# Perceiver layer on one core: turned probabilities spread by sixteen SBUF-to-SBUF transfers instead of through a DRAM buffer

## The reference, cut to what matters

```
x = x + cross_attention(layernorm(x), ctx)     # 256 queries, 25088 context rows, width 512
x = x + attention(layernorm(x))                # 16 heads
x = x + ffn(layernorm(x))                      # shared expert + 1 of 32 routed experts per token

scores   = einsum('bqh,bkh->bqk', Q_char, K_sub) * scale      # 256 x 25088
char2sub = einsum('bqk,bkh->bqh', softmax(scores), V_sub)
```

## Time and profile before

| | |
|---|---|
| time, median of 3 executions | 1302.32 us (1300.58 to 1302.76) |
| the profiled execution | 1300.58 us, its span 1298.8 us |
| mean granted TensorE clock | 0.957 |
| PE busy / DVE / ACT | 85% / 45% / 30% of the span |
| the loop over pairs, first `spread` to last | 74.89 to 660.92 us of the span |

### The profile page before, as it was taken

How to read it: one execution, slowest core, us unless ns; L and a number is a source line. 1 busy time by engine, 2 the same in 40 slices (tenths; PEclk the granted TensorE clock), 3 DMA queues, 4 the chain that set the end, 5 groups by cost and what they waited for, 6 DMA issues and landing times.

```text
span 1298.8 us, 16532 instructions
## 1 busy us (share of the span) xinstructions
PE 1105.0 (85%) x6586; PEld 750.9 (58%) x6586; DVE 582.5 (45%) x859; ACT 392.5 (30%) x621; POOL 3.5 (0%) x20
## 2 busy tenths in 40 slices
PE   8999888998999899999889989999886675665666
PEld 8777666776777777777666945766332222222223
DVE  2466666776776777677664245421110010010101
ACT  1245434554553554455441225211110000000000
POOL 1000000000000000000000000000000000000000
PEclk9999999999999999999989989999998989889998
DMA  9168887787777877878762811897899999999996
GB/s 357 59 227 291 278 276 278 236 253 253 267 239 247 281 235 230 280 236 255 258 227 103 351 66 33 342 422 304 360 423 423 423 422 419 420 423 425 420 422 284
DMA packets 102063, 381.42 MB, mean 294 GB/s; under 512 B 5521, under 2 KB 5649, under 8 KB 89617
## 3 DMA queue, kind: packets, MB, share of 16 engines
q1 hardware_dynamic: 102032, 381.00, 78.7%
HBM read 355.29 MB, written 25.69 MB: 293 GB/s over the span
## 4 chain that ended last, share of the span: by engine, by line
PE 29%; DMA 28%; SPq 22%; DVE 12%; issue 5%; ACT 4%; DVEq 0%
SPq L410 13%; DMA nat<-in_ctx_rows 11%; DMA strips<-turned 8%; DVE ctt_lo L1151 4%; SPq L412 3%; DMA ctt<-in_ctx_t 3%; DVE turned L1183 3%; ACT nat_hi L935 3%; DMA wd<-in_r_down 3%; SPq L334 2%; DMA wu<-in_r_up 2%; PE ps L807 2%; DVE st L1168 2%; PE ps L875 2%; PE ps L885 2%
## 5 line engine op out<-in xcount | busy, mean ns | idle before, releaser
L560 PE MATMUL ps<-nat_hi,pt_hi 128*128 128x512 f32 x384 | 159.1, 414 | 50.2 <-DVE pt_lo L1161 50.2
L547 PE MATMUL ps<-ctt_hi,q_hi 128*128 128x512 f32 x392 | 156.2, 398 | 3.2 <-DVE ctt_lo L1151 3.2
L562 PE MATMUL ps<-nat_hi,pt_lo 128*128 128x512 f32 x384 | 157.4, 410 | 0.0
L561 PE MATMUL ps<-nat_lo,pt_hi 128*128 128x512 f32 x384 | 156.9, 409 | 0.0
L548 PE MATMUL ps<-ctt_lo,q_hi 128*128 128x512 f32 x392 | 155.5, 397 | 0.0
L549 PE MATMUL ps<-ctt_hi,q_lo 128*128 128x512 f32 x392 | 155.5, 397 | 0.0
L1449 DVE TENSOR_TENSOR hh<-sg,ps 128x256 f32<-128x256 f32 x32 | 13.5, 421 | 262.1 <-PE ps L851 262.1
L560 PEld LDWEIGHTS ps<-nat_hi,pt_hi 128*128 128x128 f32 x384 | 75.6, 197 | 76.6 <-issue 59.5
L1151 DVE TENSOR_TENSOR ctt_lo<-ctt,ctt_hi 128x2048 fp32r<-128x2048 f32 x49 | 112.0, 2289 | 17.3 <-ACT ctt_hi L931 17.3
L1156 DVE TENSOR_TENSOR nat_lo<-nat,nat_hi 128x2048 fp32r<-128x2048 f32 x48 | 110.0, 2292 | 17.1 <-ACT nat_hi L935 14.3
L1161 DVE TENSOR_TENSOR pt_lo<-pt,pt_hi 128x1024 fp32r<-128x1024 f32 x48 | 58.6, 1221 | 129.1 <-ACT pt_hi L939 129.1
(11 more groups left out here) (265 smaller groups left out, 1238.4 us busy)
## 6 DMA issues: line engine op xcount, KB each, us to landing
wu<-in_r_up SPq DMA_DIRECT2D x32, 2048.0 KB, 30.3
wd<-in_r_down SPq DMA_DIRECT2D x32, 2048.0 KB, 33.9
wg<-in_r_gate SPq DMA_DIRECT2D x31, 2048.0 KB, 36.5
ctt<-in_ctx_t SPq DMA_DIRECT2D x49, 1024.0 KB, 8.9
nat<-in_ctx_rows SPq DMA_DIRECT2D x48, 1024.0 KB, 7.2
strips<-turned SPq DMA_DIRECT2D x96, 256.0 KB, 4.4
pt<-strips SPq DMA_DIRECT2D x24, 1024.0 KB, 4.8
w_gate<-in_w_g_t SPq DMA_DIRECT2D x2, 1024.0 KB, 10.9
```

Of the source, the lines that this page charges most:

```text
L547: mm(o, qh, ctt_hi[par][:, c, :], start=(c == 0), stop=False)
L560: mm(o, p_hi[:, w, :], n_hi[:, t, :], start=(first and t == 0), stop=False)
L561: mm(o, p_hi[:, w, :], n_lo[:, t, :], start=False, stop=False)
L562: last = mm(o, p_lo[:, w, :], n_hi[:, t, :], start=False, stop=(final and t == KT - 1))
```

## The change

`strips` and its semaphore go. `spread(u)` now issues sixteen transfers of 64 KB (32 partitions, 2 KB of each), one for each pair (g, k), directly from `turned` to `pt`. They all count on `pt_loaded`, and ACT waits for all sixteen. No wait is left inside `spread`.

ACT and DVE take their work in another order: the high and low parts of `nat[1]` now stand ahead of those of the second half of `pt`, and on DVE the maximum of the first score block stands ahead of the first `probs_lo`. ACT's wait on `products_done` before the second `probs_hi` is dropped; the load of `nat[1]`, for which ACT waits just before, is itself issued only after that count.

```diff
             def spread(u):
                 sp.wait_ge(s["turned_ready"], u * 2 + 2)
                 for g in range(G):
-                    sp.dma_start(strips.rearrange("(k j) g n -> j k g n", k=G)[:, :, g, :],
-                                 turned[g * Q:(g + 1) * Q, :, :, :, :].rearrange("j k h w i -> j k (h w i)")
-                                 ).then_inc(s["strips_stored"], 16)
-                sp.wait_ge(s["strips_stored"], u * (16 * G) + 16 * G)
-                sp.dma_start(pt[:, :, :, :, :].rearrange("p g h w i -> p (g h w i)"), strips.rearrange("p g n -> p (g n)")
-                             ).then_inc(s["pt_loaded"], 16)
+                    for k in range(G):
+                        sp.dma_start(pt[k * Q:(k + 1) * Q, g, :, :, :], turned[g * Q:(g + 1) * Q, k, :, :, :]
+                                     ).then_inc(s["pt_loaded"], 16)
...
             def probs_hi(u, half):
-                act.wait_ge(s["pt_loaded"], u * 16 + 16)
+                act.wait_ge(s["pt_loaded"], u * (16 * G * G) + 16 * G * G)
...
-            def pair(u, par, first=False, last=False):
+            def pair(u, par, last=False):
 
                 rows_hi(u - 1, 0)
                 probs_hi(u - 1, 0)
-                if not first:
-                    act.wait_ge(s["products_done"], u * 2 - 2)
+                rows_hi(u - 1, 1)
                 probs_hi(u - 1, 1)
-                rows_hi(u - 1, 1)
...
                 rows_lo(u * 2 - 2, nat[0], nat_hi[0], nat_lo[0])
+                block_max(u * 2, 0)
                 probs_lo(u * 2 - 2, 0)
-                block_max(u * 2, 0)
+                rows_lo(u * 2 - 1, nat[1], nat_hi[1], nat_lo[1])
                 probs_lo(u * 2 - 1, 1)
-                rows_lo(u * 2 - 1, nat[1], nat_hi[1], nat_lo[1])
                 step(block_max(u * 2 + 1, 1))
...
             rows_lo(NB - 3, nat[0], nat_hi[0], nat_lo[0])
-            probs_lo(NB - 3, 0)
             step(block_max(NB - 1, 0))
             pair_bias(0, halves=1)
+            probs_lo(NB - 3, 0)
+            rows_lo(NB - 2, nat[1], nat_hi[1], nat_lo[1])
             probs_lo(NB - 2, 1)
-            rows_lo(NB - 2, nat[1], nat_hi[1], nat_lo[1])
```

More of the change, by code:

```diff
@@ L234, in perceiver_layer @@
         x_loaded0 x_loaded1 cols_loaded rows_loaded wqc_loaded wks_loaded wkc_loaded wqs_loaded wvc_loaded sel_loaded
-        wg2_loaded wg1_loaded wvs_loaded nat_loaded0 nat_loaded1 ctt_loaded0 ctt_loaded1 end_nat_loaded strips_stored pt_loaded watt_loaded wo_loaded
+        wg2_loaded wg1_loaded wvs_loaded nat_loaded0 nat_loaded1 ctt_loaded0 ctt_loaded1 end_nat_loaded pt_loaded watt_loaded wo_loaded
         gw_loaded0 gw_loaded1 gw_loaded2 uw_loaded0 uw_loaded1 uw_loaded2 dw_loaded0 dw_loaded1 dw_loaded2
@@ L275, in perceiver_layer @@
         var, sd, newt = cell(76, 2), cell(78, 2), cell(58, 2)
-        strips = nc.dram_tensor("strips", (P, G, 2 * QT * KT * Q), F32, kind="Internal").ap()
         block = ctx.enter_context(nc.Block())
@@ L997, in _ @@
             act.wait_ge(s["gate2_in_psum"], 1)
-            pair(1, 1, first=True)
+            pair(1, 1)
             with act.Fori(1, NS // 2 - 1) as i:
@@ L1005, in _ @@
             probs_hi(NS - 1, 0)
-            act.wait_ge(s["products_done"], NB - 3)
-            probs_hi(NS - 1, 1)
             exps(NS, 0, halves=1)
             rows_hi(NS - 1, 1)
+            probs_hi(NS - 1, 1)
             act.wait_ge(s["end_nat_loaded"], 16)
```

## The result

| | before | after |
|---|---|---|
| median | 1302.54 us | 1359.13 us (1355.6 to 1360.28) |
| ratio | | 1.043, 95% interval 1.0403 to 1.0456 |
| span of the profiled execution | 1298.8 us | 1353.8 us |
| HBM written | 25.69 MB | 0.52 MB |
| steady period of the loop (19 of them) | 24.96 us | 27.58 us |

The forecast was 1299.6 us, the range 1277 to 1335. The traffic went away as written, and the kernel lost 57 us.

What follows compares the result with a forecast made beforehand. The prediction took the ring SP, DMA, ACT, DVE, SP, not PE, to bound the loop. Steady periods +2.3, three early periods -3.1 and the end -1.9 sum to -2.7 us: 1302.32 becomes 1299.6 us, range 1277 to 1335.

Steps and rivals of the forecast that it cites:

- The ring: Loop's chain of waits from one spread through `nat[1]`, ACT and DVE to the next: 24.95 us before, 25.07 forecast.
- part 1: Spread start to issue of `nat[1]`: sixteen issues at 0.47 a step make 7.68 us instead of 6.79, 0.89 more.
- The upper bound: Spread start to issue of `nat[1]`: at most 11.8 us, from 0.72 for each issue, the mean of the four stores.
- Rival 1: Sixteen issues: each transfer costs its own time whatever its size; 0.72 a step, 1395 us in all; chance 0.25.
- The price rule: Issue step in the spreads: it counts 345 times, so 0.01 us of step is worth 3.5 us.
- Part 2: Transfer of `nat[1]` in the loop: 5.5 us instead of 7.42, 1.92 less, with the load of `pt` gone.
- Part 3: DVE's order: the second `pt_lo` now stands between `nat_lo` and the second maximum, adding 1.15 us to the ring.
- Part 5: Three periods before 186.61, where the chain goes through the `ctt` load: -1.04 us each, -3.1 us in all.
- Part 6: End of the loop, where PE waits for `pt`: it lands after 9.06 us instead of 10.94, -1.9 us.
- Rival 2: Ring loses about 1.2 us a period: moved `pt_lo` off it (1278) or issues at 0.38 (1271); chance 0.15.
- rival 3: No savings before 186.61 and at the end, only the steady periods' 2.3 us more: 1304.6 us; chance 0.10.

Runs made afterwards that it cites:

- The probe: The changed kernel with groups of six transfers of different shapes added behind the store of the output, to time SP's issues; one execution took 1419.47 us.
- e3_nat1_first: The changed kernel with the load of `nat[1]` and its wait on the products ahead of the sixteen transfers in SP's queue; 1347.91 us, 1.0348 of before.
- e9_split_old_order: The changed kernel with the sixteen transfers split over SP's and ACT's queues and ACT's and DVE's order of before; 1232.52 us, 0.9469 of before.

## Why the prediction was wrong

- **The ring was right.** The prediction read from the earlier trace rows that the loop is bound by SP, DMA, `nat[1]`, ACT, DVE, SP and not by PE. The chain after shows the same ring, and four variants (26.35, 26.10, 24.31, 22.64 us a period) came within 0.1 of what it gives.
- **The step that failed is part 1, the size of the issue.** I took 0.47 a step from the earlier trace rows, "one issue takes 0.42 to 0.43". It is 0.63. All rows of before have an end in DRAM; none shows an issue with both ends in SBUF, which was exactly the new thing. 15 x 0.16 is 2.4 of the 2.5 us by which this part was off, and 23 such spreads make 57 us, nearly all of the miss (1359.1 - 1299.6 = 59.5).
- **The upper bound held, its weight did not.** Rival 1 was right in kind ("each transfer costs a time of its own, whatever its size"), and its 0.72 a step was above the 0.63. Its number for the time, 1395, was 36 us too high. But I argued the rival down with bytes ("they carry 256 KB each, and the new ones a quarter of that"). The probe shows that between SBUF and SBUF bytes do not count, 0.59 for 16 KB and 0.60 for 256 KB, so the argument was wrong. The price rule in it was good: 0.01 us of step is worth 3.5 us, and 0.16 x 345 = 55 us. The range should have reached the end of this bound, since the step counts 345 times in the result.
- **Part 2, the transfer of `nat[1]`:** 5.43 against 5.5, right. The small transfers do not drag behind it, and the last lands 2.0 us after its issue, with one issued every 0.63: they overlap. The estimate from the 0.95 us for 64 KB of the Trainium skill's page "DMA: Bandwidth & Descriptors" (Bandwidth), taken one after the other, did not come: `nat[1]` landed 15.6 us after the start of the spread and not 21.
- **Part 3, the moved `pt_lo`:** 1.15 forecast; 1.14 and 1.23 measured in the two kernels made for it. Right.
- **Part 5, the first three long periods:** -1.04 forecast for each; they grew from 28.4 to 30.3 us in the mean. (The period before these three, 26.6 us, which the prediction left out, became 25.7.) The queue did get shorter: `nat[1]` to `ctt` landed took 154.58 - 141.18 = 13.4 instead of 15.2, 1.8 of the 1.92 forecast. The issue ate it, 10.4 instead of 7.43.
- **Part 6, the end:** -1.9 forecast, +0.2 measured. The landing after the last issue was right (2.07 against 2.1); the last issue started at 9.42 instead of 6.96.
- **Rival 2** (the moved `pt_lo` not on the ring, or issues at 0.38) and **rival 3** did not happen.

## What to carry to other kernels

Find the ring that sets a loop's period before pricing a change: here PE was 85% busy and still had 2.5 us of slack in each period, and what stood behind what in SP's queue decided. A queue's issue time is a resource with a count: multiply it by the number of issues that stand ahead of the next transfer that someone waits for, and price it from a row with the same kind of ends, or bound it wide. When issues are what counts, split them over two queues before giving up the change: the same sixteen transfers went from 4.3% slower to 5.3% faster, half of the issues moved and the order of ACT and DVE taken back.

## What the runs showed of the hardware that was not expected

- Issuing a DMA with both ends in SBUF takes SP 0.59 to 0.61 us (0.63 to the next start), for 32 as for 128 partitions and for 16 KB as for 256 KB. With one end in DRAM most issues take 0.42 to 0.43 (0.47), but the first two stores of the shape of `strips` in the probe took 0.61 and 0.60. Where the extra 0.16 us comes from was not tried and stays open.
- SP and ACT issue at the same time: 8 in 4.97 us and 8 in 5.30 us over the same stretch, SP at the 0.63 a step that it has alone.
- Stores of the shape of `strips` (32 partitions, four pieces of 2 KB each to DRAM) hold SP for 0.69 and 1.30 us at the third and fourth, with nothing else running. Why is open.
- After an idle stretch of 3.3 us in each period read of `e3_nat1_first`, TensorE started at the lower of its two levels, matmuls 0.43 us apart instead of 0.23, for about 3 us; in `e9_split_old_order`, where PE waits for 1.3 us in all in the steady periods, the granted clock was 1.00 through the whole loop.
